# The output of an attention unit: bank copied whole by ACT, reciprocals multiplied in on POOL

## The reference, cut to what matters

```
B, T, M, D, G, H = 4, 1024, 512, 128, 4, 4
q = rope(einsum('bim,ghmd->bghid', x, w_aq))
k = rope(einsum('bim,gmd->bgid', x, w_ak))
v = einsum('bim,gmd->bgid', x, w_av)
s = einsum('bghid,bgjd->bghij', q * c, k * c) - 1e30 * (i < j)
p = softmax(s, axis=-1)
o = einsum('bghij,bgjd->bghid', p, v)
r = einsum('bghid,ghdm->bim', o, w_ao)
```

## Time and profile before

| what | value |
| --- | --- |
| median of three runs | 3738.14 us (3728.04 to 3741.01) |
| the profiled execution | 3748.78 us, of which the span from first to last instruction is 3747.0 us |
| PE busy | 3419.2 us, 91% of the span |
| DVE, POOL, ACT busy | 2189.7, 1743.5, 1623.2 us |
| loop of the attention | from 44 us to about 2490 us |
| mean granted clock of TensorE | 0.971 |

### The profile page before, as it was taken

One profiled execution on the slowest core, in us unless ns is written; L12 is line 12 of the kernel. 1 busy time (PEld: TensorE's weight loads), 2 busy tenths in 40 slices (PEclk: granted clock), 3 DMA queues, 4 the chain that ended last, 5 costly groups with the idle time before them and its releaser, 6 DMA issues. The chain is left out here.

```text
span 3747.0 us, 73872 instructions
## 1 busy us (share of the span) xinstructions
PE 3419.2 (91%) x20373; PEld 2915.2 (78%) x20375; DVE 2189.7 (58%) x4740; ACT 1623.2 (43%) x3672; POOL 1743.5 (47%) x2208
## 2 busy tenths in 40 slices
PE   6999999999999999999999999966998999999987
PEld 5888888888888788888888888864786777777766
DVE  6665665656656566566565665656663444444448
ACT  2543544435445354354543544532123444444443
POOL 2544435444344353443544435456223555555548
PEclk9999999999999999999999999987998999999999
DMA  2211103102112111110311102126324777767767
GB/s 84 63 33 37 54 21 120 55 27 63 27 50 93 48 62 35 38 52 24 102 63 36 54 24 62 46 80 229 126 67 133 169 184 157 176 164 170 176 153 271
DMA packets 231780, 339.91 MB, mean 91 GB/s; under 512 B 20304, under 2 KB 105552, under 8 KB 230640
## 3 DMA queue, kind: packets, MB, share of 16 engines
q1 hardware_dynamic: 198128, 244.43, 20.3%
q0 software_dynamic: 33280, 91.02, 11.6%
HBM read 225.00 MB, written 110.38 MB: 90 GB/s over the span
## 5 line engine op out<-in xcount | busy, mean ns | idle before, releaser
L588 DVE TENSOR_TENSOR ptl<-TP,pth 128x512 fp32r<-128x512 f32 (+1 forms) x640 | 407.3, 636 | 255.5 <-ACT pth L746 245.6
L746 ACT CAST pth<-TP 128x512 fp32r<-128x512 f32 (+1 forms) x640 | 347.2, 550 | 312.7 <-PE TP L923 309.8
L838 PE MATMUL O<-pth,vh 128*128 128x256 f32 (+1 forms) x1280 | 402.9, 315 | 26.8 <-DVE ptl L588 23.6
L576 DVE TENSOR_REDUCE negmax<-S 128x1 f32<-128x384 f32 (+7 forms) x512 | 379.3, 747 | 22.7 <-PE S L908 16.9
L838 PE MATMUL S<-kTh,qTh 128*128 128x512 f32 (+3 forms) x768 | 308.2, 401 | 67.2 <-ACT prob L738 29.3
L404 POOL TENSOR_TENSOR work<-work,cst 128x320 f32<-128x320 f32 x128 | 132.9, 1038 | 501.7 <-ACT work L730 501.7
L840 PE MATMUL O<-pth,vl 128*128 128x256 f32 (+1 forms) x1280 | 359.7, 281 | 0.0
L839 PE MATMUL O<-ptl,vh 128*128 128x256 f32 (+1 forms) x1280 | 359.5, 281 | 0.0
L838 PE MATMUL S<-wph,xTh 128*128 128x512 f32 (+1 forms) x1024 | 353.8, 346 | 3.5 <-issue 1.7
L1674 POOL DMA_INDIRECT acc_d<-yb,idy x144 | 229.4, 1593 | 255.7 <-ACT yb L1725 237.8
L839 PE MATMUL S<-wpl,xTh 128*128 128x512 f32 (+1 forms) x1024 | 346.3, 338 | 0.0
(11 more groups left out here) (320 smaller groups left out, 9433.3 us busy)
## 6 DMA issues: line engine op xcount, KB each, us to landing
raww<-in_L_ffn_w_dram SPq DMA_DIRECT2D x33, 1024.0 KB, 7.8
stage<-in_L_attn_w_aq_dram SPq DMA_DIRECT2D x68, 256.0 KB, 3.0
raww<-in_L_ffn_w_dram SPq DMA_DIRECT2D x33, 512.0 KB, 11.2
stage<-in_L_attn_w_ao_dram SPq DMA_DIRECT2D x64, 256.0 KB, 2.6
work<-in_L_attn_x_dram SPq DMA_DIRECT2D x64, 256.0 KB, 2.8
xt_d<-work SPq DMA_DIRECT2D x64, 256.0 KB, 2.8
a<-acc_d SPq DMA_DIRECT2D x64, 256.0 KB, 3.9
h_d<-work SPq DMA_DIRECT2D x40, 256.0 KB, 3.1
```

The lines of the kernel that those rows point to most:

```text
L576: nc.vector.tensor_reduce(negmax[:, n % 4:n % 4 + 1], S[:, a, 0:(IB * ib + a + 1) * P], AX_X, ALU.max, negate=True).then_inc(max_ready, 1)
L588: nc.vector.tensor_tensor(ptl[:, n % 2, 0:w], TP[:, n % 2, 0:w], pth[:, n % 2, 0:w].bitcast(F32), ALU.subtract).then_inc(tp_lo, 1)
L746: nc.scalar.copy(pth[:, n % 2, 0:w], TP[:, n % 2, 0:w]).then_inc(tp_hi, 1)
L838: mm(out, ah, bh, start=first, stop=False)
```

## The change

ACT now copies the whole bank, 512 columns, to `onorm`, which is twice as wide. Its signal `over_ready` tells two readers at once: PE, for which the bank is free with it (`bank_free`), and POOL, which multiplies the two halves of `onorm` (SBUF by SBUF) and then rounds and subtracts as before. DVE's `norm_out` is gone. The semaphore `o_free`, which counted unit outputs and projections together, becomes `r_free`, which counts projections alone. To make room, small tiles are laid over others that are free at their time (`late` over the cosine table, for use after the loop; `vareps`, `std`, `rstd` over `lgt` before it; `top2` and `idx2` in the loop), and `negmax`, `rsum`, `rinv` become parts of one tile `sums`.

```
-        onorm = sb("onorm", [P, IB * P])
-        negmax, rsum, rinv = sb("negmax", [P, 4]), sb("rsum", [P, 4]), sb("rinv", [P, 4])
+        onorm = sb("onorm", [P, 2 * IB * P])
+        sums = sb("sums", [P, 12])
+        negmax, rsum, rinv = (sums[:, i * 4:i * 4 + 4] for i in range(3))
...
-                        wait_apart(pool, o_free, it * MG + (OUTPUTS.index(("o", u)) + 1 + 2))
-                        nc.gpsimd.tensor_scalar(slot(oTh, u), onorm[:], 1.0, 1.0, ALU.mult, ALU.mult).then_inc(o_hi, 1)
-                        pool.wait_ge(o_hi, it * len(UNITS) + u + 1)
-                        nc.gpsimd.tensor_tensor(slot(oTl, u), onorm[:], slot(oTh, u).bitcast(F32), ALU.subtract).then_inc(o_split, 1)
+                        wait_apart(pool, over_ready, it * len(UNITS) + (u + 1))
+                        out = onorm[:, 0:IB * P]
+                        nc.gpsimd.tensor_tensor(out, out, onorm[:, IB * P:2 * IB * P], ALU.mult).then_inc(o_hi, 1)
+                        wait_apart(pool, o_hi, it * (2 * len(UNITS)) + (2 * u + 1))
+                        nc.gpsimd.tensor_scalar(slot(oTh, u), out, 1.0, 1.0, ALU.mult, ALU.mult).then_inc(o_hi, 1)
+                        pool.wait_ge(o_hi, it * (2 * len(UNITS)) + (2 * u + 2))
+                        nc.gpsimd.tensor_tensor(slot(oTl, u), out, slot(oTh, u).bitcast(F32), ALU.subtract).then_inc(o_split, 1)
...
-                    def norm_out(u):
-
-                        v.wait_ge(over_ready, it * len(UNITS) + u + 1)
-                        nc.vector.tensor_tensor(onorm[:], bank("o", u)[:, 0:IB * P], onorm[:],
-                                                ALU.mult).then_inc(o_free, 1)
...
                         beside(u)
-                        norm_out(u)
                     add_results(PROJECT_LAST)
...
                         act.wait_ge(o_split, it * len(UNITS) + u + 1)
-                        nc.scalar.copy(onorm[:], bank("o", u)[:, IB * P:2 * IB * P]).then_inc(over_ready, 1)
+                        nc.scalar.copy(onorm[:], bank("o", u)).then_inc(over_ready, 1)
...
+            def bank_free(kind, n, it):
+
+                k = OUTPUTS.index((kind, n))
+                if k < 2:
+                    pe.wait_ge(r_free, it * NT + 1)
+                elif OUTPUTS[k - 2][0] == "o":
+                    pe.wait_ge(over_ready, it * len(UNITS) + (OUTPUTS[k - 2][1] + 1))
+                else:
+                    pe.wait_ge(r_free, it * NT + (PROJECTED.index(OUTPUTS[k - 2][1]) + 2))
...
                         if jp == 0:
-                            pe.wait_ge(o_free, m0 + (OUTPUTS.index(("o", u)) + 1))
+                            bank_free("o", u, it)
...
                         ib, a = t // IB, t % IB
-                        pe.wait_ge(o_free, m0 + (OUTPUTS.index(("r", t)) + 1))
+                        bank_free("r", t, it)
```

More of the change, by code:

```diff
@@ L142, in attention @@
         mv = sb("mv", [P, NT, 2])
-        vareps, std, rstd = sb("vareps", [P, NT]), sb("std", [P, NT]), sb("rstd", [P, NT])
         half = sb("half", [P, 1])
-        mvh, fsc, fsh, fmr = sb("mvh", [P, NT, 2]), sb("fsc", [P, NT, 3]), sb("fsh", [P, NT, 6]), sb("fmr", [P, NT, 2])
+        late = cst[:, C_COS:C_COS + 29 * NT]
         stx, st1 = sb("stx", [P, 2, 6]), sb("st1", [P, 2, 6])
@@ L148, in attention @@
         scx, scr, sch, mr = sb("scx", [P, 2, 3]), sb("scr", [P, 2, 3]), sb("sch", [P, 2, 6]), sb("mr", [P, 2, 2])
-        onorm = sb("onorm", [P, IB * P])
-        negmax, rsum, rinv = sb("negmax", [P, 4]), sb("rsum", [P, 4]), sb("rinv", [P, 4])
-        top8, idx8 = sb("top8", [P, NT, 8]), sb("idx8", [P, NT, 8], U32)
+        onorm = sb("onorm", [P, 2 * IB * P])
+        sums = sb("sums", [P, 12])
+        negmax, rsum, rinv = (sums[:, i * 4:i * 4 + 4] for i in range(3))
+        top2, idx2 = sb("top2", [P, 2, 8]), sb("idx2", [P, 2, 8], U32)
         S = ctx.enter_context(nc.psum_tensor("S", [P, 2, 1024], F32))
@@ L173, in attention @@
         ident = cst[:, C_ID:C_ID + P]
+        mvh, fsc, fsh, fmr, top8, idx8 = (late[:, a * NT:b * NT].rearrange("p (t c) -> p t c", t=NT)
+                                          for a, b in ((0, 2), (2, 5), (5, 11), (11, 13), (13, 21), (21, 29)))
+        idx8 = idx8.bitcast(U32)
+        vareps, std, rstd = (lgt[:].rearrange("p s e -> p (s e)")[:, i * NT:(i + 1) * NT] for i in range(3))
         cos = cst[:, C_COS:C_COS + NT * HALF].rearrange("p (t c) -> p t c", t=NT)
@@ L210, in attention @@
         o_split = sem("o_split")
-        o_free = sem("o_free")
+        r_free = sem("r_free")
         r_done = sem("r_done")
@@ L317, in _ @@
                     iteration(b, g)
-                sp.wait_ge(o_free, b * (G * MG) + (G * MG + 2))
+                sp.wait_ge(r_free, b * (G * NT) + (G * NT + 1))
                 sp.dma_start(r_d[b].rearrange("(t p) m -> p t m", p=P), racc[:]).then_inc(r_out, 16)
@@ L478, in _ @@
             v.sem_inc(tp_lo, 2)
-            v.sem_inc(o_free, 2)
+            v.sem_inc(r_free, 1)
             for name in (xt_out, x2_out, h_out):
@@ L510, in root @@
             def root(src, eps, scale, base, k, roots):
-                nc.vector.tensor_scalar(vareps[:], src, scale, eps, ALU.mult, ALU.add).then_inc(var_ready, 1)
+                nc.vector.tensor_scalar(vareps, src, scale, eps, ALU.mult, ALU.add).then_inc(var_ready, 1)
                 v.wait_ge(std_ready, roots)
-                return link(nc.vector.reciprocal(rstd[:], std[:]), base, k)
+                return link(nc.vector.reciprocal(rstd, std), base, k)
             def center(t, src, dst):
@@ L600, in add_results @@
                             if copies:
-                                nc.vector.tensor_copy(racc[:, t], bank("r", t)).then_inc(o_free, 1)
+                                nc.vector.tensor_copy(racc[:, t], bank("r", t)).then_inc(r_free, 1)
                             else:
-                                nc.vector.tensor_tensor(racc[:, t], racc[:, t], bank("r", t), ALU.add).then_inc(o_free, 1)
+                                nc.vector.tensor_tensor(racc[:, t], racc[:, t], bank("r", t), ALU.add).then_inc(r_free, 1)
                     def step(ins, n):
@@ L629, in beside @@
                             wait_apart(v, xp_hi, it * SIDE + (3 * k + 4))
-                            step(nc.vector.max(top8[:, k], lgt[:, k]), 2 * k + 7)
-                            nc.vector.max_index(idx8[:, k], top8[:, k], lgt[:, k]).then_inc(dl, 1)
+                            step(nc.vector.max(top2[:, k], lgt[:, k]), 2 * k + 7)
+                            nc.vector.max_index(idx2[:, k], top2[:, k], lgt[:, k]).then_inc(dl, 1)
                     lo_tile(NT - 3)
@@ L676, in linked @@
                 v.wait_ge(dl, ZD + sums[0])
-            v.wait_ge(o_free, B * G * MG + 2)
+            v.wait_ge(r_free, N * NT + 1)
             for i in range(NT + 4):
@@ L708, in _ @@
             act.wait_ge(var_ready, 1)
-            nc.scalar.activation(std[:], vareps[:], ACT.Sqrt).then_inc(std_ready, 1)
+            nc.scalar.activation(std, vareps, ACT.Sqrt).then_inc(std_ready, 1)
             act.sem_inc(xp_hi, 1)
@@ L778, in beside @@
                             wait_apart(act, dl, it * 10 + (2 * k + 8))
-                            nc.scalar.copy(coef[:, bass.ds(tile + k, 1), 0:K], top8[:, k:k + 1, 0:K])
-                            nc.scalar.copy(topi[:, bass.ds(tile + k, 1), :], idx8[:, k:k + 1, 0:K])
+                            nc.scalar.copy(coef[:, bass.ds(tile + k, 1), 0:K], top2[:, k:k + 1, 0:K])
+                            nc.scalar.copy(topi[:, bass.ds(tile + k, 1), :], idx2[:, k:k + 1, 0:K])
                             nc.scalar.copy(coef[:, bass.ds(tile + k, 1), K:K + 2], mr[:, k:k + 1])
@@ L829, in _ @@
                     nc.scalar.copy(lgt[:, i % 2], O[:, i % 2, 0:E]).then_inc(tp_hi, 1)
-            nc.scalar.copy(coef[:, (B - 1) * NT:B * NT, K:K + 2], fmr[:])
+            nc.scalar.copy(coef[:, (B - 1) * NT:B * NT, K:K + 2], fmr)
         @block.tensor
@@ L858, in _ @@
                     tp0 = pe.snap(it * TG + NT)
-                    m0 = pe.snap(it * MG)
                     def project(t):
```

## The result

The changed kernel takes 3785.61 us (median; 3774.24 to 3786.35), the kernel before 3739.57 us beside it: a ratio of 1.0129, 95% interval 1.0114 to 1.0145, so 43 to 54 us slower. The profiled execution took 3785.25 us, with a span of 3783.4 us. Against the 3747.0 us before that is only 36 us more, because the profiled execution of before lay 13 us above the median of all its later runs (3735.9). TensorE's mean granted clock was 0.971 in it; of the later runs the three at 0.971 took 3743.5 to 3751.8 us, and the one at 0.979 took 3725.1. I therefore compare places within an iteration, and not spans.

A forecast was written before the change was run, and what follows sets the result against it. PE, 91% busy, was taken as the bound, waiting on a closed ACT-DVE chain. Per iteration 1.00 (copies) + 1.65 (POOL) - 0.20 (bank freed sooner) = 2.45 us; over 16 iterations 39 us, giving 3777 us; 8-in-10 range 3741 to 3796.

The forecast's parts named there:

- The mechanism up to the bank of unit 7: Units 0 to 7: ACT's later copies and POOL's longer work delay PE's projection of tile 3, 2.45 us an iteration.
- ACT's wider copy: Chain of units 0 to 5: each copy holds ACT's queue 0.47 us, not 0.25, adding 0.20 us to the chain.
- POOL's multiplication: POOL, each output: 0.74 us plus 0.19 us waiting for its result; the scale at unit 7 comes 1.65 us later.
- The bank is freed sooner: Unit 7's bank: ACT's copy itself frees it for PE, 0.66 us instead of 0.86, so 0.20 sooner.
- The sum at this place: PE's wait for unit 7's bank: 1.00 + 1.65 - 0.20 = 2.45 us later per iteration.
- DVE's relief: DVE loses about 108 us of busy time with no gain for PE, since the subtraction still waits for ACT's cast.
- the copies have room: Second half of each iteration: ACT often waits for PE, so nothing is added to or given back from the delay.
- third rival: Second half: ACT's copies wait for POOL's late split; two 0.93 us waits on PE's path, 3807 us; chance about 0.04.
- the waits for side tiles: PE's 32 waits for tiles ACT copies out of S would grow from 0.74 us each to 1.1.
- the wait for the bank: PE's wait at the projection of tile 3 would grow to about 1.4 us per iteration, some 22 us in all.
- ACT's at L776: ACT's wait for POOL's scale at unit 7's normalization would grow from 0.50 us to about 2.

The follow-up runs named there:

- e_half: Changed kernel with ACT copying only the output's 256 columns and POOL multiplying by a constant, so the division by row sums is left out: 3739.83 us.
- e_defer: Changed kernel with ACT's copies of units 0 to 5 moved behind the next unit's cast (two casts after even units): 3757.72 us.
- e_swap: Changed kernel with ACT's copy of unit 7's bank put ahead of the normalization that waits for POOL's scale: 3769.45 us.
- e_dve: Changed kernel with the multiplication back on DVE, from SBUF, while ACT still copies the whole bank: 3760.22 us.
- e_nomul: Changed kernel with POOL's multiplication left out, so outputs stay undivided: 3738.14 us.
- e_late14: Changed kernel with ACT's copy of unit 14's bank moved behind the second cast of unit 15: 3767.63 us.
- v_after: Changed kernel with ACT's copies of units 0 to 5 and 14 behind the next casts, and unit 7's ahead of the normalization: 3724.98 us.

## Why the prediction was right

The forecast of 39 us lies a little below the measured 43 to 54, and the measured time lies within the stated range. The mechanism up to the bank of unit 7 is the one that the runs show; one place behind it was missed. Step by step:

- **ACT's wider copy** holds the queue for 1026.17 - 1025.71 = 0.46 us (0.47 was taken from another line), and the subtraction behind it is 0.20 us later, as taken. The copy of unit 5 is 1.04 us late (31.26 against 30.22 us from unit 0's end; 1.00 predicted), PE at unit 6 1.21 to 1.25 (1.20). e_half and e_defer show that this is the copy's width and place.
- **POOL's multiplication** takes 0.734 us (0.74) and its wait 0.16 to 0.17 (0.19). The row of the subtraction was a good guide. By the ratio of the Trainium skill's "GPSIMD Engine Reference", section 3.1, the multiplication would have taken an estimated 0.83 us, more than the trace shows. From ACT's copy of unit 5 to L776 it is 1060.89 - 1049.29 = 11.60 us against 10.11, 1.49 more (1.65). POOL's longer work doesn't slow its neighbours: DVE's subtractions take 691 and 555 ns on average, by shape, in both traces, and ACT's casts 591 and 487.
- **The bank is freed sooner**: 1062.22 - 1061.61 = 0.61 us from copy to PE, 0.25 less than before (0.20). The sum at this place is 44.19 - 41.91 = 2.28 us against 2.45, and e_swap shows that it hangs on the order of L776 and the copy.
- **DVE's relief is worth nothing**: 101 us less busy, and in the chain 0.03 us an iteration behind the narrow copy (e_half) and 0.06 behind the wide one (e_dve against e_nomul).
- **Behind that place** one step failed: "in the second half ... the copies have room". The copy of unit 14 had 0.19 us. Unit 14 is short; POOL's multiplication makes the split of unit 13 late, the copy waits 0.39 us for it, and the cast and the subtraction behind it are late for PE: 0.63 us an iteration. This is the third rival's mechanism; it reaches PE at one place and not at two, and is smaller than its price. e_late14 takes exactly this away.

That the forecast came so near is in part luck: the sum up to the bank was 0.17 us too large, 0.15 us more is given back up to unit 13, and the 0.63 us of unit 14, which it took as nothing, go the other way.

The predicted signs came as said, smaller: the waits for side tiles grew to 0.94 us each (1.1), the wait for the bank to 19.7 us (22), ACT's at L776 to 1.7 us on average (2). Not foreseen were the 48 new waits for DVE's low part: 32 of them are a part of the chain's delay, and 16 belong to the copy of unit 14, since they are gone in e_late14.

The loop explains 16 x 2.54 = 41 us, from the median distance of unit 0 from one iteration to the next (154.68 against 152.14). What the measured difference has beyond that, 2 to 13 us, no run here settles. Behind the loop the traces show no loss: from unit 15 of the last iteration to the end it is 1271 us before and 1270 after, and 1261 to 1268 in the six experiments that divide their outputs. The other part of the change, small tiles laid over others, was never undone by itself.

## What to carry to other kernels

Relieving a busy engine gains nothing where its work stood beside another engine's that ends at the same time; ask first what the next instruction waits for. A copy that nobody needs soon must not stand ahead of a cast that a chain needs now: moving such copies in the queue won 61 us here (v_after against the changed kernel), more than the 46 that the change had lost. And when work goes to an idle engine, follow everything behind it in that engine's queue, to each short unit whose successor waits for it.

## What the runs showed that I had not expected

Leaving the division out changed the time of the experts' stage, 142 scatters in place of 144: an experiment that changes values in a kernel that routes by them can only be read in the stage before the routing. And the profiled execution of the kernel before was 13 us slower than its median, more than a quarter of the effect.
